# Local attention on one core: 192 columns of probabilities per head instead of 256, three transposes per pair of heads instead of four, edge rows of V brought by transfers

## The reference, cut to what matters

```python
def local_attention(q, k, v):                 # WINDOW = 128, QK_SCALE = 8
    w = n // WINDOW
    bq = q.reshape(b, h, w, WINDOW, d) * QK_SCALE
    ...                                       # bk, bv: the window before, and the own one
    sim = jnp.einsum('bhwid,bhwjd->bhwij', bq, bk)
    mask = (i < j) | (i > j + WINDOW) | (j == -1)
    sim = jnp.where(mask, -jnp.finfo(sim.dtype).max, sim)
    attn = jax.nn.softmax(sim, axis=-1)
    out = jnp.einsum('bhwij,bhwjd->bhwid', attn, bv)
```

## Time and profile before

| | |
|---|---|
| median of 3 runs | 1915.9 us |
| the profiled execution | 1916.24 us, of it the span of its instructions 1914.2 us |
| PE busy over the span | 1841.3 us (96%) |
| DVE, ACT, POOL busy | 1512.0, 1102.2, 432.2 us |

### The profile page before, as it was taken

How to read it: one execution, slowest core, us unless ns; L and a number is a source line. 1 busy time by engine, 2 the same in 40 slices (tenths; PEclk the granted TensorE clock), 3 DMA queues, 4 the chain that set the end, 5 groups by cost and what they waited for, 6 DMA issues and landing times. The chain is left out here.

```text
span 1914.2 us, 44588 instructions
## 1 busy us (share of the span) xinstructions
PE 1841.3 (96%) x15388; PEld 1612.0 (84%) x15388; DVE 1512.0 (79%) x4715; ACT 1102.2 (58%) x2551; POOL 432.2 (23%) x319
## 2 busy tenths in 40 slices
PE   8899999999999799999999899989999999989998
PEld 8789889889889588888888788867888888868887
DVE  6888878878778688888888677768888888877777
ACT  4433433433433388888888444437888888853333
POOL 0000000000000244454444000014554545411111
PEclk9999999999999799999999999998999999999999
DMA  9100000000010100000000200010000000000002
GB/s 344 49 1 1 1 1 1 1 1 1 1 69 1 51 6 5 5 4 5 5 5 11 87 12 11 11 45 4 6 4 5 5 5 5 4 23 12 11 11 93
DMA packets 44983, 44.51 MB, mean 23 GB/s; under 512 B 8359, under 2 KB 39387, under 8 KB 44894
## 3 DMA queue, kind: packets, MB, share of 16 engines
q1 hardware_dynamic: 44894, 43.33, 6.9%
HBM read 34.93 MB, written 8.39 MB: 23 GB/s over the span
## 5 line engine op out<-in xcount | busy, mean ns | idle before, releaser
L1117 ACT ACTIVATE l_probs<-l_probs,l_negmax 128x256 f32<-128x256 f32 x512 | 253.1, 496 | 83.3 <-DVE l_negmax L1227 83.3
L1075 POOL TENSOR_TENSOR l_t<-l_t,l_rnorm 128x512 f32<-128x512 f32 x128 | 131.0, 1044 | 295.3 <-DVE l_rnorm L1244 295.3
L1070 POOL TENSOR_TENSOR l_t<-l_t,l_t 128x1024 f32<-128x1024 f32 x64 | 153.2, 2393 | 129.0 <-DVE l_t L1279 129.0
L117 PE MATMUL ps<-local_w_hi,l_xT 128*128 128x512 f32 x384 | 167.7, 437 | 9.0 <-DVE l_t L1279 3.3
L118 PE MATMUL ps<-local_w_lo,l_xT 128*128 128x512 f32 x384 | 153.7, 400 | 0.0
L486 ACT ACTIVATE attn_exp<-ps 128x512 f32<-128x512 f32 x128 | 76.4, 599 | 133.2 <-PE ps L119 133.2
L119 PE MATMUL ps<-local_w_hi,l_xT 128*128 128x512 f32 x384 | 153.1, 399 | 0.0
L1405 PE MATMUL ps<-ident,l_probs 128*128 128x128 f32 x1024 | 145.7, 279 | 1.6 <-ACT l_probs L1117 1.4
L117 PE MATMUL ps<-m_hnT_hi,ffn_w_hi 128*128 128x512 f32 (+1 forms) x352 | 142.4, 405 | 4.3 <-PEq L1017 4.3
L118 PE MATMUL ps<-m_hnT_lo,ffn_w_hi 128*128 128x512 f32 (+1 forms) x352 | 139.6, 396 | 0.0
L119 PE MATMUL ps<-m_hnT_hi,ffn_w_lo 128*128 128x512 f32 (+1 forms) x352 | 139.6, 396 | 0.0
(11 more groups left out here) (252 smaller groups left out, 5774.5 us busy)
## 6 DMA issues: line engine op xcount, KB each, us to landing
tok_x<-x SPq DMA_DIRECT2D x16, 512.0 KB, 7.9
m_shifted<-shifted SPq DMA_DIRECT2D x20, 256.0 KB, 2.8
shifted<-x SPq DMA_DIRECT2D x64, 64.0 KB, 1.5
out<-x SPq DMA_DIRECT2D x8, 512.0 KB, 4.2
ffn_w_raw<-ffn_w SPq DMA_DIRECT2D x6, 640.0 KB
local_w_raw<-ffn_wqkv SPq DMA_DIRECT2D x4, 768.0 KB, 5.6
tok_base<-attn_base SPq DMA_DIRECT2D x4, 512.0 KB, 8.6
h<-txt SPq DMA_DIRECT2D x4, 512.0 KB, 8.4
```

Source lines behind the costliest of these rows:

```text
L117: nc.tensor.matmul(out, wh, mh, start=start, stop=False, skip_group_check=True)
L1070: nc.gpsimd.tensor_tensor(t1[:], t1[:], t2[:], ALU.add).then_inc(s.summed.sem, 1)
L1075: nc.gpsimd.tensor_tensor(v, v, rn[:, a * LH:(a + 1) * LH].unsqueeze(2).to_broadcast([P, LH, DH]), ALU.mult).then_inc(s.rotated.sem, 1)
L1117: last = nc.scalar.activation(v, v, ACT.Exp, bias=nb[:, h:h + 1], scale=-1.0, accum_out=rsum[:, h:h + 1])
```

## The change

- **Layout of the probabilities.** Per pair and query row there are 384 columns instead of 512 (`REACH` = 192 per head), mirrored: head 0 has its main block (128 keys) in columns 0 to 127 and its edge (64 keys) in 128 to 191; head 1 its edge in 192 to 255 and its main block in 256 to 383. For the lower 64 queries the main block is the window before and the edge the lower 64 tokens of the own window; for the upper 64 queries the main block is the own window and the edge the upper 64 tokens of the window before.
- **score** therefore always works in pieces of 128 and 64 keys: 32 products per tile; before, every second tile had 16 products of 192 keys and the others 32 of 128 and 64.
- **VectorE and ScalarE** handle 192 columns per head (maxima, exponentials), and `probs_out` copies 384 columns per pair.
- **probs_t** has three transposes per pair; the middle one turns both edges at once: 64 keys of head 0 in partitions 0 to 63, 64 of head 1 in 64 to 127.
- **values** needs the edge rows of V in the same partitions: a new tile `edge` [128, 2, 512] has head 0's features in the lower partitions, head 1's in the upper ones and zeros elsewhere (a memset per layer). ScalarE's copy of V orders the features by head parity, and SP moves, per tile, 2 x 2 pieces of 64 rows x 256 features (64 KB) from V to `edge`: the own tile's lower rows after `v_done`, its upper rows (for the next tile) after `o_full`. Per tile there are 32 products of 64 columns instead of 16 of 128, and a new wait for `edged`.
- **The mask** for even tiles is rebuilt over 320 columns as sel * flag + mask in one operation; two masks of 128 x 320 are loaded instead of four of 128 x 128.

```diff
+            def edge_of(which, w, tokens):
+                for e, rows in enumerate((LOW, HIGH)):
+                    cols = slice(e * LINNER // 2, (e + 1) * LINNER // 2)
+                    sp.dma_start(edge[rows, which, cols], vv[tokens, w, cols]).then_inc(s.edged.sem, 16)
+            def own_edge(t, w):
+                sp.wait_ge(*s.v_done.after(t + 1))
+                edge_of(0, w, LOW)
+            def next_edge(t, w):
+                sp.wait_ge(*s.o_full.after(t + 1))
+                edge_of(1, w, HIGH)
             with sp.Fori(0, T // 2 - 2) as p:
                 for r in range(2):
+                    own_edge(2 * p + 1 + r, 1 - r)
                     store(p, r)
+                    next_edge(2 * p + 1 + r, 1 - r)
...
+            nc.gpsimd.memset(edge[:], 0.0).then_inc(s.set.sem, 1)
...
-                nc.scalar.activation(pt[:, pair], ps[:, PT[pair]], ACT.Copy).then_inc(s.p_done.sem, 1)
+                nc.scalar.activation(pt[:, pair], ps[:, PT[pair], 0:2 * REACH], ACT.Copy).then_inc(s.p_done.sem, 1)
...
-                    nc.scalar.activation(vv[:, r], ps[:, V], ACT.Copy).then_inc(s.v_done.sem, 1)
+                    nc.scalar.activation(vv[:, r].rearrange("p (e m d) -> p m e d", e=2, d=DH),
+                                         ps[:, V].rearrange("p (m e d) -> p m e d", e=2, d=DH),
+                                         ACT.Copy).then_inc(s.v_done.sem, 1)
...
-                    pm[:, pair, e * 2 * P:(e + 1) * 2 * P], ps[:, bank, at:at + 2 * P],
-                    mask[:], -8.0, -LOWEST, ALU.add, ALU.min, nb[:, h:h + 1])
+                    pm[:, pair, e * REACH:(e + 1) * REACH], ps[:, bank, at:at + REACH],
+                    mask[:, e * P:e * P + REACH], -8.0, -LOWEST, ALU.add, ALU.min, nb[:, h:h + 1])
...
-                    chain(nc.vector.tensor_scalar(mask_e[:, P:2 * P], prev[:], negs[:, bass.ds((n - 1) // 2, 1)], None,
-                                                  ALU.add))
+                    chain(nc.vector.scalar_tensor_tensor(mask_e[:], before_sel[:], negs[:, bass.ds((n - 1) // 2, 1)],
+                                                         mask_o[:], ALU.mult, ALU.add))
...
             def score(half, own):
+                parts = (((1 - own, slice(0, P)), (own, slice(0, P))), ((own, LOW), (1 - own, HIGH)))
+                places = ((0, DH), (P, 0))
...
             def probs_t(t, pair):
                 wait(pe, s.exped, 4 * t + pair + 1)
-                for k in range(4):
+                for k in range(3):
...
+            def values(own):
                 for pair in range(LPAIRS):
+                    for half, w in enumerate((1 - own, own)):
+                        tokens = slice(half * DH, (half + 1) * DH)
+                        for kind in range(2):
+                            for e in range(2):
+                                at = e * LINNER // 2 + pair * DH
+                                keys, block = ((vv[:, w, at:at + DH], 2 * e), (edge[:, half, at:at + DH], 1))[kind]
+                                last = nc.tensor.matmul(ps[e * DH:(e + 1) * DH, OT, pair * P + tokens.start:pair * P + tokens.stop],
+                                                        keys, pt[:, pair, block * P + tokens.start:block * P + tokens.stop],
+                                                        start=(kind == 0), stop=(kind == 1))
...
                     wait(pe, s.v_done, n - 1)
+                    wait(pe, s.edged, 64 * (n - 2) + 32)
                     wait(pe, s.y_done, n - 2)
```

More of the change, by code:

```diff
@@ L970, in local_phase @@
     HF = DH // 2
+    REACH = K.REACH
+    LOW, HIGH = slice(0, DH), slice(DH, P)
     ms = K.mlp_s[layer]
[L972 removed]
+    (xc, xt, sq, t1, t2, qt, kt, vv, edge, pm, pt, on, spread, oth, otl), at = mem.place(
         K.mlp_end, mem.end, (f"l{layer}_x", [P, 2, D], F32),
@@ L1381, in score @@
                 bank = QK if half == 0 else TQ
-                reach = (((slice(0, 3 * DH),), (slice(DH, 4 * DH),)) if own else
-                         ((slice(2 * DH, 4 * DH), slice(0, DH)), (slice(0, 2 * DH), slice(3 * DH, 4 * DH))))
+                parts = (((1 - own, slice(0, P)), (own, slice(0, P))), ((own, LOW), (1 - own, HIGH)))
+                places = ((0, DH), (P, 0))
                 for pair in (2 * half, 2 * half + 1):
[L1385 to L1388, removed]
+                    for part, place in zip(parts, places):
+                        for qs, (w, keys) in zip((LOW, HIGH), part):
                             for e in range(2):
+                                at = pair % 2 * 2 * P + place[e]
                                 rows = slice(e * DH, (e + 1) * DH)
-                                last = nc.tensor.matmul(ps[qs, bank + e, at + keys.start:at + keys.stop], qt[rows, pair, qs],
-                                                        kt[rows, pair].rearrange("p w t -> p (w t)")[:, keys],
+                                last = nc.tensor.matmul(ps[qs, bank + e, at:at + keys.stop - keys.start],
+                                                        qt[rows, pair, qs], kt[rows, pair, w, keys],
                                                         start=True, stop=True)
@@ L1407, in probs_t @@
                 last.then_inc(s.p_t.sem, 1)
-            def values():
+            def values(own):
                 for pair in range(LPAIRS):
[L1412 to L1416, removed]
-                                                    pt[:, pair, (2 * e + w) * P:(2 * e + w + 1) * P],
-                                                    start=(w == 0), stop=(w == 1))
+                    for half, w in enumerate((1 - own, own)):
[7 more added lines that the diff above has]
+                                                        start=(kind == 0), stop=(kind == 1))
                 last.then_inc(s.o_full.sem, 1)
@@ L1896, in __init__ @@
         self.scored = count("scored")
+        self.edged = count("edged")
         self.masked = count("masked")
@@ L1954, in __init__ @@
         self.ident = aps["ident"]
-        self.mask_cur = aps["mask_cur"]
-        self.mask_prev = aps["mask_prev"]
+        self.mask = aps["mask"]
+        self.mask_sel = aps["mask_sel"]
         self.negs = aps["negs"]
@@ L2115, in build @@
         K.signs = [(K.flags[:], A.flags), (K.negs[:], A.negs)]
-        K.masks = [(K.mask_prev[:], A.mask_prev), (K.mask_o[:, P:2 * P], A.mask_cur), (K.mask_e[:, 0:P], A.mask_cur),
-                   (K.mask_o[:, 0:P], A.mask_prev)]
+        K.masks = [(K.mask_o[:], A.mask), (K.mask_sel[:], A.mask_sel)]
         def tables(layer):
@@ L2182, in arrays @@
     i, j = np.arange(P)[:, None], np.arange(P)[None, :]
-    out["mask_prev"] = np.where(i > j, MASKED, 0.0).astype(np.float32)
-    out["mask_cur"] = np.where(i < j, MASKED, 0.0).astype(np.float32)
+    prev, cur = (np.where(hidden, MASKED, 0.0).astype(np.float32) for hidden in (i > j, i < j))
+    low, high = slice(0, DH), slice(DH, P)
+    out["mask"] = np.concatenate([np.concatenate([prev[low], cur[low, low], prev[low]], 1),
+                                  np.concatenate([cur[high], prev[high, high], cur[high]], 1)])
+    edge = np.arange(2 * P + DH)[None, :] // DH == P // DH
+    out["mask_sel"] = ((i < DH) != edge).astype(np.float32)
     first = np.arange(T // 2) % (TB // 2) == 0
```

24 lines of the change are left out of this document (17 added, 7 removed).

## The result

The changed kernel takes 1920.9 us (median of 9 runs, 1919.4 to 1924.0) against 1915.7 of the kernel before beside it (9 runs, 1912.4 to 1917.3): ratio 1.0032, 95% interval 1.0021 to 1.0042. It is slower by some 5 us; the forecast was 1918 with a range of 1911.5 to 1927. The profiled execution's span is 1918.5 us against 1914.2.

A forecast was written before the change was run, and what follows sets the result against it. PE, 96% busy, was taken to wait in each loop step for ACT's chain ending in the V copy. Terms of +0.10 us a step (+6.0 over 60), fill and drain -3.8, masks -0.2 gave +2.0: 1918, range 1911.5 to 1927.

The forecast's parts named there:

- Gate, four transposes worth 0: Loop step: ACT's copy of V, not the last transpose, holds PE's V projection, so four transposes less gain 0.
- Copy of V in another order, 0: ACT's V copy, written in pieces of 64, costs 0; 0 to +0.02 us per step for the range.
- Scores, +0.02: Odd tiles' scores become 64 narrower records: +0.04 us on every second step, +0.02 on average.
- Values, +0.08: Values stage: 16 more groups at 5 ns each, +0.08 us per step, from 1.90 to 1.98.
- Rival C: Values: narrow groups cost 10 ns each instead of 5, 0.16 us per step; 1924 in all; 27%.
- rival B: Values: two heads' weight loads go one behind the other, +1.67 us per step and tile; 2020 in all; 6%.
- The new wait, 0: Values' wait for edge transfers costs 0, as they start 5.2 us after the V copy ends; range up to 0.5 per layer.
- Fill and drain with masks, -4.0: Outside the loop: narrower maxima and exponentials give -3.8 us in all, loading fewer masks -0.2.
- The sum: Whole kernel: +6.0 us over 60 loop steps, -3.8 fill and drain, -0.2 masks: net +2.0, 1918 us.
- no difference: Total time: a difference within 0.2% (3.8 us) can't be told from none; 52%.
- slower: Total time: slower by more than 0.2% (3.8 us); 36%.
- narrower maxima and exponentials: DVE's and ACT's work over fewer columns: 0 in the loop, where neither is last; counts only in fill and drain.

The follow-up runs named there:

- values in halves: Kernel before with every product of values cut into two of 64 columns, no edge transfers: 1924.1 us, ratio 1.0046.
- two moved blocks: Changed kernel with ACT's V copy ahead of the squares and PE's V projection ahead of the transposes of pairs 2 and 3: 1894.3 us, ratio 0.9884.
- the same moves without the change: Kernel before with V copy ahead of squares and V projection ahead of pairs 2 and 3, 24 transposes, wide products in values: 1929.1 us, ratio 1.0063.
- the kernel with both moves and three transposes: Kernel before with V copy ahead of squares, V projection ahead of pairs 2 and 3, and three transposes per pair: 1934.3 us, ratio 1.0096.

## Why the prediction was right, and where its size was off

- **Gate, four transposes worth 0.** Right. The V projection starts 0.06 after the V copy, 0.15 after the last transpose; 2.98 against 2.99 us. Three transposes alone changed nothing, and with the copy earlier the step fell by 0.147, of which 0.12 are PE's new wait in front of the V projection.
- **Copy of V in another order, 0.** Right: 0.62 us as before.
- **Scores, +0.02.** Right: 1.50 on every tile.
- **Values, +0.08.** This is the step that was mis-sized: +0.13 was measured (1.90 to 2.03 on average). The rate was nearly right, the count was not. The prediction spread the scores' 0.04 us over the 8 groups that are added there, and took 16 added groups for values. But what costs more than its columns is a narrow group: 58.5 against 54.5, 4 ns each. The scores have 8 narrow ones beside 8 of 128 columns, 8 x 4 = 0.03 to the 0.04 measured; in values all 32 are narrow, 32 x 4 = 0.128, or 8 ns for each group added. Rival C had the argument (all 32 in a row are narrow), its price of 0.16 was 0.03 too high where mine was 0.05 too low. Bound from above, loads in a row (+1.7, rival B), is refuted: 2.03 us. Its price of 53 ns for a load of 64 columns more (190 - 137) was misread too: the transposes' loads (L1405) have the same 128 x 128 and are recorded with 140, so the 190 of L848 can't be put down to the number of columns.
- **The new wait, 0.** Right; transfers land after 2.0 us (median of 252), and without them the time is the same.
- **Fill and drain with masks, -4.0.** Right in the main. The loops cost 60 x 0.151 = +9.1. The two local phases, from the first q/k product to the last product of y, grew from 429.3 to 431.9 us and from 429.3 to 432.5, +5.7 together, so fill and drain gave -3.4 (predicted -3.8). The span grew by 4.3 only; the other -1.3 lies outside the local phases, where the change does nothing but load its masks, and is the clock's, as far as can be seen: behind each local phase the profile before has a stretch of 3.4 us at the lower clock that the profile after has not. The second is below, before first, and is worth 1.7 us; for the first, 1065 to 1100 us has a granted clock of 0.95 before and 1.00 after. (The profile after is in turn at the lower clock for 3.4 us longer around 1278 us, where the second phase begins.) The runs give about the same total: values in halves +0.46%, 8.8 us; with the scores' 1.2 the changed kernel should be at +10.0, it is at +0.32% or 6.1: -3.9. The waits shrank as read: in front of the projection in the fill from 0.99 to 0.72 (predicted 0.27 less), in the drain from 2.59 to 1.91 (0.68, predicted 0.54).

```profile
1708.00:1712.00 4.00, 4.00 (x13) 3.13 (x11) 0.87 (x4) 0.90 (x2) 0.00 (x0) 0.57 0.44 128
```

```profile
1708.00:1712.00 4.00, 1.70 (x12) 1.50 (x12) 3.63 (x6) 1.26 (x2) 0.00 (x0) 1.00 0.04 12
```

```profile
659.09 0.77 PE L117 MATMUL ps<-local_w_hi,l_xT 128*128 128x512 f32 x1 [0.72 <-DVE l_negmax L1259]
...
1046.68 0.63 PE L1430 MATMUL ps<-ident,l_t 128*128 128x128 f32 x4 [1.91 <-POOL l_t L1105]
```

- **The sum.** +2.0 predicted, +5 measured. The 0.05 us a step by which values were too small, 60 times, are 3 us: the size of the miss. That nothing else moved the total is in part luck: clock stretches of 1 to 2 us aren't in the sum. The miss put the difference on the other side of what a measurement can tell: 52% were given to "no difference", 36% to "slower".
- **What the prediction didn't see.** It counted narrower maxima and exponentials as 0 in the loop, since DVE and ACT weren't last. That holds for this order. But they are the part of the change with worth in it: with ACT's order changed they decide 0.57 us a step, while the transposes, the part that PE's 96% draws the eye to, changed no step in the two pairs of kernels that differ in them and the copies behind them alone (12.67 and 12.68; 12.85 and 12.85).

## What to carry to other kernels

Before counting what a change removes, find the instruction that starts last before the work goes on, and ask from whose end it starts. An engine busy 96% can be waiting inside that number. A cost per instruction is multiplied by the instructions that have the new size, not by those that were added. If a change saves work on engines that aren't last, reorder so that the saving meets the wait: here two moved blocks turned +0.3% into -1.2%, and the same moves without the change gave +0.6%.

## What the hardware showed that was not expected

- Products of two heads side by side (128 rows by 64 columns of weights each) take 109 ns for 128 moving columns, 58.5 for 64, and about 58 for 32: there is a floor just above the streaming time of 64 columns.
- In front of the loop's jump back values take 2.04 to 2.08 us, in the other steps 2.015. That the jump is the cause isn't shown. It appears with narrow products only (1.90 in all steps before), with and without edge transfers.
- Stretches at the lower clock behind a local phase are there in one kernel and not in another, whose work there is the same; the one shown is worth 1.7 us, and in the kernel with both moves and three transposes the stretch from 1045 to 1085 us lost at most 5 against its neighbour (0.13 of 40 us). Differences of that size between single profiles aren't the change's.
- An operation of DVE on 16 columns ends 0.03 to 0.04 us after POOL's addition in every loop step of six traces, though the program has no wait between them; it is recorded with up to 1.13 us instead of 0.17.
